# Attention output transposes one step later, probabilities and exponentials eight at a time, and other PSUM banks for the feed-forward bursts

## The reference, cut to what matters

```python
h = shift_token(x)
q, k, v = jnp.split(h @ wqkv, 3, axis=-1)        # 8 heads of 64
q = l2norm(q) * qs; k = l2norm(k) * ksc
q, k = rotary_xpos(q, k)
o = local_attention(q, k, v)                     # windows of 64, own and previous
x = x + o @ wo
h = shift_token(x)
h = layernorm(h) * lg + lb
a, g = jnp.split(h @ w1 + b1, 2, axis=-1)        # 341 + 341 columns
x = x + (a * gelu(g)) @ w2 + b2
```

## Time and profile before

| | |
|---|---|
| median of 3 runs | 1783.23 us (1782.45 to 1784.5) |
| profiled execution, its own time | 1786.46 us |
| span of the profiled execution | 1784.7 us |
| mean granted clock of TensorE | 0.969 of full speed |
| PE busy | 1515.6 us (85%) |
| PEld busy | 1233.3 us (69%) |
| DVE busy | 1358.0 us (76%) |
| ACT busy | 1139.9 us (64%) |
| POOL busy | 1095.8 us (61%) |

### The profile page before, as it was taken

The page is one execution under the profiler, slowest core; times in us unless marked ns, Lnnn a source line. Parts: engine busy times, 40 slices in busy tenths (PEclk is TensorE's granted clock), DMA queues, the critical chain, the costliest instruction groups (busy, mean ns, idle before and its releaser), DMA issues.

```text
span 1784.7 us, 44020 instructions
## 1 busy us (share of the span) xinstructions
PE 1515.6 (85%) x15864; PEld 1233.3 (69%) x15864; DVE 1358.0 (76%) x3516; ACT 1139.9 (64%) x2364; POOL 1095.8 (61%) x1106
## 2 busy tenths in 40 slices
PE   1789999978999899977888889989998889999974
PEld 1577777766777777755666667777776777777763
DVE  6687878768787978767776479787977687979772
ACT  1576767667686767634455467676766576767671
POOL 3676868577585858623333278585857485858560
PEclk9899999989999999988999999999999999999996
DMA  8231212132221222113100132121223221212113
GB/s 284 50 122 43 57 41 62 48 95 50 68 51 48 51 71 51 40 29 122 36 25 21 46 96 54 45 54 45 63 57 87 59 60 44 54 44 54 45 28 119
DMA packets 183670, 112.46 MB, mean 63 GB/s; under 512 B 86720, under 2 KB 164128, under 8 KB 182944
## 3 DMA queue, kind: packets, MB, share of 16 engines
q1 hardware_dynamic: 183456, 109.65, 23.5%
HBM read 43.41 MB, written 23.42 MB: 37 GB/s over the span
## 4 chain that ended last, share of the span: by engine, by line
PE 50%; DVE 26%; ACT 9%; issue 7%; SPq 3%; DMA 2%; POOL 1%; DVEq 0%; ACTq 0%; POOLq 0%
PE QK L389 9%; PE TO L639 8%; PE QK L639 5%; PE TO L706 5%; DVE rope_c L1154 5%; DVE rope_s L1159 4%; DVE o_n L1179 4%; DVE top L1098 3%; PE SC L680 3%; ACT probs L1303 3%; PE TO L389 3%; PE TO L752 3%; DVE h2n L1166 3%; PE TO L808 2%; PE VB L808 2%
## 5 line engine op out<-in xcount | busy, mean ns | idle before, releaser
L1303 ACT ACTIVATE probs<-SC,shift,qgain 128x128 f32<-128x128 f32 x1024 | 390.6, 481 | 101.9 <-DVE shift L1106 101.6
L1481 POOL TENSOR_TENSOR ve<-mv,epsilon 128x1 f32<-128x1 f32 x128 | 24.5, 192 | 392.8 <-DVE mv L1145 392.8
L389 PE MATMUL QK<-w_qkv,hT 128*128 128x512 f32 x768 | 220.7, 424 | 25.5 <-DMA w_qkv<-qkv_d 12.0
L1154 DVE TENSOR_TENSOR rope_c<-QK,rope 128x512 f32<-128x512 f32 x256 | 175.7, 686 | 80.5 <-PE QK L389 78.1
L1494 POOL TENSOR_TENSOR rnorm<-clip,mhalf 128x8 f32<-128x8 f32 x128 | 211.1, 1649 | 12.4 <-DVE clip L1115 12.2
L1503 POOL TENSOR_TENSOR qgain<-clip,mhalf 128x8 f32<-128x8 f32 x128 | 209.5, 1637 | 0.0
L639 PE MATMUL TO<-ident,probs 128*128 128x128 f32 x1280 | 189.9, 276 | 12.0 <-ACT probs L1303 11.1
L1098 DVE TENSOR_REDUCE top<-SC 128x4 f32<-128x512 f32 x256 | 174.8, 683 | 31.1 <-PE SC L680 30.9
L1297 ACT ACTIVATE v_own<-VB 128x512 f32<-128x512 f32 x128 | 76.5, 598 | 189.2 <-PE VB L389 189.2
L1159 DVE TENSOR_TENSOR rope_s<-QK,rope 128x256 f32<-128x256 f32 x512 | 191.0, 415 | 0.0
L639 PEld LDWEIGHTS TO<-ident,probs 128*128 128x128 f32 x1280 | 153.8, 142 | 45.0 <-issue 24.8
(11 more groups left out here) (174 smaller groups left out, 3745.0 us busy)
## 6 DMA issues: line engine op xcount, KB each, us to landing
v_prev<-v_own SPq DMA_DIRECT2D x256, 130.0 KB, 2.3
x_att<-stream SPq DMA_DIRECT2D x128, 64.0 KB, 2.2
h<-stream SPq DMA_DIRECT2D x256, 32.0 KB, 1.9
stream<-x_new SPq DMA_DIRECT2D x32, 256.0 KB
w_qkv<-qkv_d SPq DMA_DIRECT2D x3, 1536.0 KB, 7.5
h<-x_mid SPq DMA_DIRECT2D x128, 32.0 KB
h<-x_mid SPq DMA_DIRECT2D x128, 31.8 KB
rope<-rope_d SPq DMA_DIRECT2D x24, 128.0 KB, 3.2
```

What stands on the lines that cost most here:

```text
L389: last = mm(dst, fr(left(a)), fr(right(b)), start=(k == 0), stop=(k == 2))
L1154: v.tensor_tensor(qk(rope_c[:])[:, m], src, rope[:, i, m, 0:1, :].to_broadcast([P, HEADS, DH]), ALU.mult)
L1303: last = nc.scalar.activation(probs[:, b, hd, :], SC[:, hd * P:hd * P + P], ACT.Exp, bias=shift[:, b, hd:hd + 1], scale=qgain[:, b, hd % 4 ...
```

## The change

The order of the work in a step is written anew, on four engines. Nothing is computed otherwise, and no instruction is added or dropped.

- PE: the four transposes of `o_n` leave the end of the ATT step (behind PV and the transposes of `h` and `h2n`) and stand in the next step, as part of WO, behind the transposes of k and q. The product with `w_o` moves from ahead of the product for q and k to behind it. The first four transposes of the probabilities move from the start of the step to just ahead of the other four.
- ACT: the copy `oT` moves with the transposes, behind `kT` and `qT`. All eight exponentials of a tile stand behind it, in the ATT step; in a step with a burst they stand at its end, behind the Gelus.
- DVE: the subtractions `hT` and `h2T` move ahead of the second `highest` and `shifted`, and the sum of squares `norm2` to the end of the step, or, in a burst, ahead of the third multiply.
- POOL: `rnorm` moves to the front, `x_b2` to the back.
- The burst: even pairs use `QK` and odd ones `TT` (it was the other way round), and the second half of `w_2` goes into the first bank of `TT` and no longer into `OB`.

The banks of the burst:

```diff
         def banks(k):
-            src = TT if k % 2 == 0 else QK
+            src = QK if k % 2 == 0 else TT
```

PE, in a step:

```diff
-                    if t := tile(ATT):
-                        probs_transposed(t, 0)
                     if t := tile(WO):
-                        if t.i == 0:
-                            pe.wait_ge(s_wow, t.loads() * 16)
-                        pe.wait_ge(s_oT, t.count())
-                        if before is not None:
-                            pe.wait_ge(s_xn, before * 2 + 2)
+                        pe.wait_ge(s_on, t.count())
                         for c in range(PAIRS):
-                            last = mm(OB[:, 0:DIM], oT[:, c, :], w_o[:, c, :], start=(c == 0), stop=(c == PAIRS - 1))
-                        last.then_inc(s_y, 1)
+                            last = transpose(OB[:, c * P:c * P + P], o_n[:, c * P:c * P + P])
+                        last.then_inc(s_to, 1)
...
+                    if t := tile(WO):
+                        if t.i == 0:
+                            pe.wait_ge(s_wow, t.loads() * 16)
+                        pe.wait_ge(s_oT, t.count())
+                        for c in range(PAIRS):
+                            last = mm(OB[:, 0:DIM], oT[:, c, :], w_o[:, c, :], start=(c == 0), stop=(c == PAIRS - 1))
+                        last.then_inc(s_y, 1)
...
                         product(mm, VB[:], lambda x: hT[:, b, x, :], lambda x: w_qkv[:, x, 1024:1536]).then_inc(s_v, 1)
                     if t := tile(ATT):
+                        if before is not None:
+                            pe.wait_ge(s_xn, before * 2 + 2)
+                        probs_transposed(t, 0)
+                    if t := tile(ATT):
...
-                        need(pe, s_on, t.count(back=1))
                         probs_transposed(t, 1)
...
-                    if t := tile(ATT):
-                        pe.wait_ge(s_on, t.count())
-                        for c in range(PAIRS):
-                            last = transpose(OB[:, c * P:c * P + P], o_n[:, c * P:c * P + P])
-                        last.then_inc(s_to, 1)
```

PE, in a burst (`w1_pair`, `w2_half`):

```diff
-                    if k == 1 and n == ITERS - 1:
+                    if k == 1 and (t := tile(ATT)):
+                        pe.wait_ge(s_on, t.count())
+                    if k == 0 and n == ITERS - 1:
                         pe.wait_ge(g_z, TILES)
-                    if k == 1 and (t := tile(QKV)):
+                    if k == 0 and (t := tile(QKV)):
                         pe.wait_ge(s_rot, t.count())
                         pe.wait_ge(s_sq, t.count())
...
-                    dst = VB if half == 0 else OB
+                    dst = VB if half == 0 else TT
...
-                    elif t := tile(ATT):
-                        pe.wait_ge(s_oT, t.count())
```

DVE, in a step (`squares_summed` holds the three lines taken out here):

```diff
-                if t := tile(TQK):
-                    highest(t, 1)
-                    shifted(t, 1)
-                if t := tile(QKV):
-                    b = t.i % 2
-                    dve.wait_ge(s_sq, t.count())
-                    need(dve, s_rn, t.count(back=2))
-                    v.tensor_reduce(norm2[:, b, :], sq[:].rearrange("p (h d) -> p h d", d=DH), AX, ALU.add).then_inc(s_n2, 1)
...
+                if t := tile(TQK):
+                    highest(t, 1)
+                    shifted(t, 1)
+                if burst is None and (t := tile(QKV)):
+                    squares_summed(t)
...
                     for k in range(6):
+                        if k == 2 and (t := tile(QKV)):
+                            squares_summed(t)
```

ACT, in a step:

```diff
-                if t := tile(ATT):
+                if t := tile(WO):
+                    act.wait_ge(s_to, t.count())
+                    need(act, s_y, t.count(back=1))
+                    copy(oT[:], OB[:].rearrange("d (c t) -> d c t", c=PAIRS)).then_inc(s_oT, 1)
+                if before is None and (t := tile(ATT)):
+                    need(act, s_tp, t.count(back=2, unit=2))
+                    exponentials(t, 0)
                     exponentials(t, 1)
...
-                if t := tile(TQK):
-                    need(act, s_tp, t.count(back=2, unit=2))
-                    exponentials(t, 0)
...
+                    if t := tile(TQK):
+                        need(act, s_tp, t.count(back=2, unit=2))
+                        exponentials(t, 0)
+                        exponentials(t, 1)
```

More of the change, by code:

```diff
@@ L723, in f @@
                                     lambda x: w_qkv[:, x, m * 512:m * 512 + 512]).then_inc(signal, 1)
+                    if t := tile(WO):
[5 more added lines that the diff above has]
+                        last.then_inc(s_y, 1)
+                    if t := tile(QKV):
+                        b = t.i % 2
                         if t2 := tile(FFN_IN + 1):
@@ L1107, in shifted, with squares_summed @@
                                        in1=qgain[:, t.i % 2, :].rearrange("p (c e) -> p e c", e=2)[:, half], op0=ALU.mult, op1=ALU.mult).then_inc(s_sh, 1)
+            def squares_summed(t):
+                b = t.i % 2
+                dve.wait_ge(s_sq, t.count())
+                need(dve, s_rn, t.count(back=2))
+                v.tensor_reduce(norm2[:, b, :], sq[:].rearrange("p (h d) -> p h d", d=DH), AX, ALU.add).then_inc(s_n2, 1)
             def clipped(t):
@@ L1127, in step @@
                             dve.wait_ge(s_st, before * 32 + 16)
-                        src = (VB if half == 0 else OB)[:, :].rearrange("p (t c) -> p t c", t=HALF)
+                        src = (VB[:] if half == 0 else TT[:, 0:512]).rearrange("p (t c) -> p t c", t=HALF)
                         v.tensor_tensor(x_new[:, half * HALF:half * HALF + HALF, :], src,
@@ L1346, in step @@
                     copy(fr(h2T[:, 0, t.i * P:t.i * P + P]), VB[:, P:2 * P]).then_inc(s_h2T, 1)
-                if t := tile(ATT):
-                    act.wait_ge(s_to, t.count())
-                    need(act, s_y, t.count(back=1))
-                    copy(oT[:], OB[:].rearrange("d (c t) -> d c t", c=PAIRS)).then_inc(s_oT, 1)
                 if burst is not None:
@@ L1477, in step @@
             def step(tile, burst, before):
+                if t := tile(QKV + 1):
+                    b = t.i % 2
+                    pool.wait_ge(s_cl, t.count(unit=2) - 1)
+                    g.tensor_tensor(rnorm[:, b, :], clip2[:, b, 8:16], mhalf[:, 0:8], ALU.pow).then_inc(s_rn, 1)
                 if t := tile(FFN_IN):
@@ L1483, in step @@
                     g.tensor_tensor(rstd2[:, b, :], ve2[:, b, :], mhalf[:, 0:1], ALU.pow).then_inc(s_rs2, 1)
-                    if i == 0:
-                        pool.wait_ge(s_ffnw, t.loads() * 96 - 15)
-                        k = t.count(back=TILES, every=TILES, unit=2)
-                        need(pool, s_xn, k)
-                    pool.wait_ge(s_xm, t.count())
-                    g.tensor_tensor(x_b2[:, i, :], x_mid[:, i, :], b_2[:], ALU.add).then_inc(s_xb2, 1)
                 if t := tile(QKV + 1):
                     b = t.i % 2
-                    pool.wait_ge(s_cl, t.count(unit=2) - 1)
-                    g.tensor_tensor(rnorm[:, b, :], clip2[:, b, 8:16], mhalf[:, 0:8], ALU.pow).then_inc(s_rn, 1)
                     pool.wait_ge(s_rn, t.count())
@@ L1510, in step @@
                     g.tensor_tensor(k_a[:], rope_c[:, 512:1024], rope_s[:, 512:1024], ALU.add).then_inc(s_ka, 1)
+                if t := tile(FFN_IN):
+                    i, b = t.i, t.i % 2
+                    if i == 0:
+                        pool.wait_ge(s_ffnw, t.loads() * 96 - 15)
+                        k = t.count(back=TILES, every=TILES, unit=2)
+                        need(pool, s_xn, k)
+                    pool.wait_ge(s_xm, t.count())
+                    g.tensor_tensor(x_b2[:, i, :], x_mid[:, i, :], b_2[:], ALU.add).then_inc(s_xb2, 1)
             def rstd_of(slot, n, moments, lot, inverse):
```

## The result

| | before | changed |
|---|---|---|
| median | 1783.87 us (1782.45 to 1787.05, 4 runs) | **1755.3 us** (1749.31 to 1756.35, 4 runs) |
| profiled execution | 1786.46 us | 1754.54 us |

The ratio is 0.9833, with a 95% interval of 0.981 to 0.9857. The kernel is faster by 28.6 us, where the forecast had 61. The direction was right and the size was not.

What follows compares the result with a forecast made beforehand. PE and DVE wait for each other, at `o_n`. Gains 47.0 + 11.2 + 8.4 = 66.6, less 4.7 for the lock, take 1786.46 to 1724.5 profiled, median 1722 us; range 1703 to 1763.

Steps and rivals of the forecast that it cites:

- The bound: PE waits 139.0 us for DVE's `o_n`, while the queued transposes of k and q do not depend on it.
- The ordinary step: Spacing of k's transposes falls from 9.17 to 8.67 us, with a new 0.57 wait ahead of QKV; 94 steps, 47.0 us.
- Does anything come later than that?: Check of `o_n`, `x_mid` to `h2n`, exponentials and POOL's 8.07: all judged to fit within the 8.67 us step.
- After a burst: Step behind a burst falls from 9.47 to 8.67 us, exponentials and table load done during `w_2`; 14 x 0.80 = 11.2 us.
- The step with the burst: Falls from 23.98 to 23.35 us, a gain of 0.63, taken as 0.6; 14 x 0.6 = 8.4 us.
- for steps in which DVE and POOL block each other (below) I take off 0.05 in each of 94, 4.7: Allowance for DVE instructions held by POOL's large ones: 4.7 us of the gain taken off.
- The lock rivals: Rivals 1 and 3, where DVE's shifts wait for POOL: 1769 us, chance 0.11, and about 1805 us, chance 0.08.
- rival 3: First shift, ahead of `o_n`, is caught by `q_r`; a caught step takes 9.65, about 1805 us; chance 0.08.
- rival 1: Second shift falls into `k_a`, closing a loop through `norm`, `clip`, `rnorm`: near 9.1 a step, 1769 us; chance 0.11.
- The late copies (2): ACT's `kT` slips 0.25 behind `hT` and `h2T`: step 8.92, 1747 us; chance 0.14.
- Rival 5: kT and qT don't hold QKV and POOL's 8.07 bounds the step: 1643 us; chance 0.04.
- Rival 4: The wait at QKV and late probabilities add up to what was saved: no gain, 1783 us; chance 0.06.

Runs made afterwards that it cites:

- 4: Changed kernel with both shifts multiplied on POOL instead of DVE, half 0 behind `q_r`, half 1 behind `k_a`, same numbers out: 1721.73 us, ratio 0.9647.
- 12: Experiment 4 with the transposes of `o_n` back at the end of the same step, behind `h2n`'s transpose: 1872.29 us, ratio 1.0499.
- 1: Changed kernel with the shift's multiplication by `qgain` left out, DVE writing the negated maximum straight into `shift`, so the output differs: 1720.72 us, ratio 0.9649.
- 11: Changed kernel with only the first shift multiplied on POOL, behind `q_r`, the second staying on DVE: 1726.21 us, ratio 0.9676.
- experiment 5: Experiment 4 with the product for v moved ahead of the product for q and k: 1720.35 us, ratio 0.9623.
- 3: Changed kernel with `ve` and `rstd` behind `qgain` in POOL's step after a burst: 1738.21 us, ratio 0.9741.
- 9: Experiment 4 with the first shift back on DVE and only the second on POOL: 1752.23 us, ratio 0.9818.
- 7: Changed kernel with the exponentials of half 0 back at the end of ACT's TQK step, ahead of `hT` and `h2T`: 1874.95 us, ratio 1.0502.
- 6: Changed kernel with POOL's old order, `ve`, `rstd`, `x_b2`, then `rnorm`: 1752.91 us, ratio 0.9814.
- experiment 10: Experiment 5 with DVE's rotation ahead of `x_mid` and `mv`: 1775.98 us, ratio 0.9951.

## Why the prediction was right in direction and off in size

**The bound** was right. The wait for `o_n` was the price, and the transposes of q and k did not need it. With the shifts off DVE (4) the wait goes from 139.0 to 5.5 us, and undone alone (12) it costs 151 us.

**The ordinary step**, 8.67 by the sum, is 8.67 wherever no held instruction is on the path, but for one of 8.83 in eight: in the changed kernel behind the burst, and in experiments 1, 4 and 11. Its terms hold too, here from experiment 4: kT 0.75 behind k's transposes, QKV at 1.90 against 1.88, the wait 0.56 behind the burst and 0.47 in the other steps against 0.57, and `x_mid` at 4.49 against 4.36. `o_n`'s transposes start at K + 1.01, earlier than the 1.15 allowed.

There is luck in it. The list of dependences ("Does anything come later than that?") leaves out the squares, which read `QK` and which k's next transposes wait for. They left PE some 0.07 us in experiment 4, and experiment 5 took away the wait that the sum counts and the step stayed. Two paths of almost one length end the step, and only one of them was priced. The second one is the way by which a late DVE reaches PE.

**After a burst**: 8.67, right. **The step with the burst** without held shifts is 23.18, where 23.35 was forecast; with them 23.87.

**The step that failed** is "for steps in which DVE and POOL block each other (below) I take off 0.05 in each of 94, 4.7". The changed kernel and experiment 4, which differ in the place of the shifts, are 1755.3 - 1721.7 = 33.6 us apart, and experiment 1, without shifts, is beside the latter; the term should have been seven times as large. Eight spacings of the two kernels tell the same: 86.2 - 84.0 = 2.1. Of that 0.69 is the step with the burst, 0.77 the second step behind it (9.44), and 0.65 the last three steps (8.75, 8.96, 8.96). Had the term been 33.6, the sum would have come to 1786.46 - 66.6 + 33.6 = 1753.5, beside 1754.54 in the profiled execution. The other terms, 66.6 together, thus hold to 3 us: they give 1719.9, and the profiled execution of experiment 4 took 1722.63. A slip beside it: 1724.5 less 3.2 is 1721.3, and the forecast says 1722.

**Why it was so small.** The lock rivals were priced as holding in every step, or in three of four, and the forecast itself took next to nothing. Each in truth costs time in some steps of every eight: rival 3 in the second step behind a burst, rival 1 in the last three and into the burst. The argument against rival 1 was that PE sets the shift's time, so that POOL would drift back until the shift falls at the end of `q_r` and is let through. The drift is real (0.28 a step in 3, 0.45 in 11). But it starts from a shift that falls into the end of `k_a`; as POOL drifts back, the shift falls nearer to `k_a`'s start, and it is held longer from step to step, until it is held whole. Then DVE has no slack (no idle row between 240.12 and 249.08) and no longer lets PE set the shift's time. In the changed kernel POOL's loop and DVE's full step are both 8.96, so the two slide together and stay. In experiment 11 POOL's loop is 9.12 and DVE's full step 207.54 - 198.71 = 8.83, and the lock undoes itself after one step. That the near equality of 8.96 and 8.96 holds it fast is read from the rows, not tested by itself.

**Which shift matters.** Taking the first off DVE brings 29 us (11), both 34 (4). The second alone brings 3 (9), which is not clear of the two kernels' intervals; there `q_r` meets the first shift more often, 50 times over 0.5 us against 21.

**The rivals.** The late copies (2) did not happen: `kT` kept its 0.75. Rival 5 was not seen; with v moved ahead (5) kT and qT hold QKV no longer, and the step stayed at 8.67. Rival 4's sum of waits was not there. The median lies inside the range of 1703 to 1763.

**The lock itself.** The trace of the changed kernel has 102 second shifts that start during a `k_a`, with a median of 1.09 us; 21 first shifts start during a `q_r`, median 1.26; and 103 start during the powers of `qgain`, a POOL instruction of 1.65 us that reads SBUF as well, at 0.16. The Trainium skill (SBUF — State Buffer, "Who interferes with whom") says that a DVE instruction with two SBUF inputs contends with a GpSimd instruction that reads SBUF. By that rule all three kinds would hold the shift. The traces agree for the 128x512 instructions and not for the powers of 128x8, so here the measurement decides.

## What to carry to other kernels

A change that lets the first engine run ahead moves every small instruction of the second against the long ones of the third; price a lock by walking several steps of both loops, not one step at a time, and look for a state in which the two loops have one length. A held instruction costs nothing until its engine's slack is used up, so ask for the slack of every path that ends in the same wait, also of those that were off the path before. A tiny two-input DVE instruction that sits ahead of critical work may be better off on the engine that it collides with: two multiplications of 128x4 a tile moved to POOL were worth 34 us of 1755 here. When a wait is moved away, ask of each other part of the change whether it is needed: here the kernel is slower than before without the move of `o_n`'s transposes (12) or without all exponentials at once (7), while POOL's new order brought nothing (6). No run puts one part alone, or the shifts' move, into the kernel before.

## What the runs showed of the hardware that was not expected

- The held instruction's row may start a little ahead of the one that holds it. In experiment 9 a shift at 232.17 was held for 1.30 us by a `q_r` at 232.18, while one at 223.48, 0.04 ahead of `q_r` at 223.52, took 0.16.
- The powers of 128x8 on POOL (1.65 us) do not hold the shift, as told above. Those shifts start 0.75 us or more into the power. In the kernel before 27 shifts start 0.30 to 0.34 into it, and take 0.16 too.
- In the one step of eight where PE's wait ahead of QKV includes a semaphore for the weights as well, QKV starts 2.06 behind k's transposes and not 1.90: 0.16 us more, and the spacing is 8.83. It is the same in the changed kernel and in experiments 1 and 4, and was not tested by itself.
- The shift is not the only small instruction that is held. In experiment 10 a `clip` of 128x8, with one input, starts at 187.81 beside a `k_a` that ends at 188.32 and takes 0.53 us; 95 of its 256 rows end 0.03 behind a `k_a` in this way. In experiment 4 nearly all of them take 0.17.
